# Both halves of a unit's value products behind the second pair of scores of the next unit, in the second layer of a two-layer transformer kernel

## The reference

```python
# retention layer, then latent attention + 4 experts (first layer), then:
q, k, v = (x @ Wq.T + bq, x @ Wk.T + bk, x @ Wv.T + bv)   # 16 heads of 8
scores = einsum('bhqd,bhkd->bhqk', q, k) * 8 ** -0.5       # not causal
scores[:, :, 0, -1] = scores[:, :, -1, 0] = -1e9
out = einsum('bhqk,bhkd->bhqd', softmax(scores), v)
x = layernorm(x + out @ Wo.T)
# then the ternary-weight projection and the last layernorm
```

## Time and profile before

| | us |
|---|---|
| median of 3 timed executions (lowest, highest) | 999.44 (997.81, 1001.86) |
| the profiled execution's own time | 990.96 |
| span of its trace | 989.2 |
| PE busy in it | 877.2 (89%) |
| DVE busy | 764.4 (77%) |
| ACT busy | 652.9 (66%) |
| mean granted TensorE clock, share of full | 0.971 |

### The profile page before, as it was taken

One profiled execution on the slowest core, in us unless ns is written; L12 is line 12 of the kernel. 1 busy time (PEld: TensorE's weight loads), 2 busy tenths in 40 slices (PEclk: granted clock), 3 DMA queues, 4 the chain that ended last, 5 costly groups with the idle time before them and its releaser, 6 DMA issues.

```text
span 989.2 us, 22910 instructions
## 1 busy us (share of the span) xinstructions
PE 877.2 (89%) x9098; PEld 440.9 (45%) x9098; DVE 764.4 (77%) x1156; ACT 652.9 (66%) x1285; POOL 390.4 (39%) x607
## 2 busy tenths in 40 slices
PE   8999899999778889988988779989989999999983
PEld 5777777778433343433734222336322222222232
DVE  4687676856687778879477588876889999999845
ACT  3555556566337777776456448765778878998981
POOL 3764677778443541236263112333441111111330
PEclk9999999999999999999989889999999999999996
DMA  8000000200500234012412410033106000100000
GB/s 304 1 2 1 1 2 1 76 1 2 154 21 23 79 120 117 23 57 74 135 35 94 122 31 23 10 111 96 46 29 178 21 20 21 39 2 3 5 22 22
DMA packets 49406, 52.53 MB, mean 53 GB/s; under 512 B 8874, under 2 KB 40618, under 8 KB 49140
## 3 DMA queue, kind: packets, MB, share of 16 engines
q1 hardware_dynamic: 45012, 48.12, 16.0%
q0 software_dynamic: 4288, 2.94, 1.1%
HBM read 32.37 MB, written 19.68 MB: 53 GB/s over the span
## 4 chain that ended last, share of the span: by engine, by line
PE 41%; DVE 27%; POOL 12%; issue 9%; ACT 6%; DMA 3%; SPq 2%; DVEq 0%; POOLq 0%; ACTq 0%
DVE arena L1980 19%; PE banks L1642 11%; PE banks L1607 7%; PE banks L1527 5%; ACT arena L1800 4%; POOL arena L383 2%; PE banks L1717 2%; PE banks L1725 2%; DMA arena<-arena 1%; PE banks L660 1%; POOL arena L896 1%; POOL arena L895 1%; PE banks L501 1%; PE banks L765 1%; POOL arena L386 1%
## 5 line engine op out<-in xcount | busy, mean ns | idle before, releaser
L1800 ACT ACTIVATE arena<-banks 128x512 f32<-128x512 f32 (+1 forms) x768 | 409.8, 588 | 110.4 <-PE banks L1607 79.9
L1980 DVE TENSOR_REDUCE arena<-banks 128x2 f32<-128x1024 f32 (+1 forms) x384 | 439.7, 1196 | 51.7 <-PE banks L1527 28.8
L1642 PE MATMUL banks<-arena 128*9 128x256 f32 (+1 forms) x3328 | 254.8, 382 | 5.8 <-ACT arena L1813 3.9
L1527 PE MATMUL banks<-arena 56*128 56x512 bf16 (+3 forms) x896 | 162.9, 366 | 29.4 <-DVE arena L1980 22.6
L1607 PE MATMUL banks<-arena 61*128 61x512 bf16 (+4 forms) x896 | 166.4, 371 | 23.6 <-ACT arena L1800 17.9
L1607 PEld LDWEIGHTS banks<-arena 61*128 61x128 bf16 (+1 forms) x896 | 44.2, 93 | 183.9 <-ACT arena L1800 157.2
L1383 POOL CAST arena<-arena 16x128 bf16<-16x128 f32 x32 | 8.9, 279 | 293.6 <-ACT arena L1868 289.6
L1642 PEld LDWEIGHTS banks<-arena 128*9 128x9 f32 x3328 | 51.4, 89 | 129.5 <-issue 82.9
L1527 PEld LDWEIGHTS banks<-arena 56*128 56x128 bf16 x896 | 45.0, 95 | 55.7 <-DVE arena L1980 44.7
L383 POOL TENSOR_TENSOR arena<-arena 128x8 f32<-128x8 f32 (+1 forms) x35 | 51.3, 1466 | 30.3 <-DVE arena L2144 27.9
L1393 POOL DMA_DIRECT2D arena<-arena x96 | 55.1, 577 | 10.7 <-POOL arena L1386 9.2
(11 more groups left out here) (243 smaller groups left out, 1428.6 us busy)
## 6 DMA issues: line engine op xcount, KB each, us to landing
arena<-k_products SPq DMA_DIRECT2D x32, 224.0 KB
arena<-q_products SPq DMA_DIRECT2D x64, 112.0 KB
q_products<-arena SPq DMA_DIRECT2D x16, 384.0 KB, 3.4
k_products<-arena SPq DMA_DIRECT2D x16, 384.0 KB, 3.7
arena<-e_w SPq DMA_DIRECT2D x22, 256.0 KB, 3.5
arena<-arena POOLq DMA_DIRECT2D x96, 4.0 KB, 1.8
sorted_rows<-c_pads SPq DMA_DIRECT2D x2, 709.5 KB, 8.5
arena<-sorted_rows SPq DMA_DIRECT2D x4, 258.0 KB, 3.1
```

Source lines behind the costliest of these rows:

```text
L1527: ins = nc.tensor.matmul(bank(first + par)[:, at:at + hi - lo], Qs[k_][rows, qc, y, qo:qo + P], Ks[k_][rows, y, lo:hi], start=True, stop=n ...
L1642: ins = nc.tensor.matmul(PS[h * VROWS:h * VROWS + VW, AV_BANK, o:end], V[:, b, kt, HG * g + h, :], Pr[u % PROBS][:, h, o:end], start=(kt = ...
L1800: s_.activation(Pr[s % PROBS][:, 2 * x + par, o:C], scores[:, o:C], ACT.Exp) \
L1980: v_.tensor_reduce(of[:, :, x], two_banks[:, :, 0:width], AX.X, ALU.max).then_inc(ring_dve, 1)
```

## The change

One condition in `order()` gets a case more. It says behind which of the two pairs of scores (`x`) of step `s` the half `y` of the value products of unit `s - 1` is put:

```diff
                     if 0 < s <= NU:
                         late = narrow(*us[s - 1])
-                        seq += [("V", (s - 1, y)) for y in range(2) if (0 if late else y) == x]
+                        seq += [("V", (s - 1, y)) for y in range(2) if (0 if late else y if us[s - 1][0] < BLOCKS else 1) == x]
```

## The result

The changed kernel takes 1037.5 us (median of 4 executions, 1033.2 to 1039.5), the kernel before beside it 1000.65 (997.8 to 1002.4). The ratio is 1.036, 95% interval 1.033 to 1.039: slower by about 36 us. In a second session both were faster, 1027.5 against 992.2, with a ratio of 1.034 (1.029 to 1.039). The forecast was 1032 in a range of 1019 to 1049.

A forecast was written before the change was run, and what follows sets the result against it. No single engine bounds the kernel; in the plain stage PE, VectorE and ScalarE are all nearly full. Terms 22.5 + 4 + 2 + 4 = +32.5 on the median 999.4 give 1032 us, range 1019 to 1049.

The forecast's parts named there:

- The gap of 1.14: Plain unit, first to second pair of scores: stays 1.14 us, held by the first exponential, with PE idle 0.53.
- The run of sixteen: Joined value products behind the second A pair: 1.06 us, saving 0.11 of PE time a unit.
- The plain unit: One second-layer unit without other work between: 2.67 us against 2.23, +0.44.
- The block and the plain stage: Eight units, 19.95 us before, become 22.4, +2.4; the stage from 744.9 to 930.3 has 9.3 such blocks, +22.5.
- The copy's delay: At a block's start, the first exponential waits behind the copy of the sums: 0.2 us a block, between 0.1 and 0.3.
- The last stage: From 930.3 to 961.6, 12 units without A pairs: +0.24 or +0.44 each, half and half, +4 us.
- The experts: From 656.6 to 695.8, 6 units: between +0.6 and +2.6 us, put at +2.
- The mixed stages: 586.9 to 656.6 and 695.8 to 744.9, 37 units: +1.6 if all waits vanish, +16 if none, put at +4 us.
- my own sign: Stated test for being wrong, one of three: the mixed stretches of the second layer take over 10 us more.
- The clock: Second layer: clock stays at 1.00 with PE busy 80% of a plain unit, so its term is 0.
- The rival of the swinging clock: Brief PE idle makes the clock swing to half in a quarter of 370 us: +33, 1065 us; chance 0.08.
- Absorption and gain: Two rivals: VectorE absorbs the gap, 999 us, chance 0.05; faster if the gap is below 0.70, 990 us, chance 0.04.

The follow-up runs named there:

- The short exponential: First of four exponentials in each second-layer unit cut to 256 of 512 columns: on the changed kernel 1.008, on the kernel before 0.998, both against the kernel before.
- the repeat: The changed kernel run and profiled once more with nothing altered, in a later session: 1027.5 us against 992.2, ratio 1.034 to the kernel before.
- the two kernels above with a changed first or fifth step alone: Kernel before, with both A pairs in a block's first gap: 1.002; or with half 0 ahead of the A pair in the step behind M: 0.997.

## Why the prediction was right

*The gap of 1.14.* Right: 1.13 to 1.14 in every unit of the plain stage but a block's first, which has 1.27 to 1.28; idle 0.53. It rested on reading a wait of 0.05 as a loop of 1.14 that was nearly covered. The short exponential moves the gap by as much as the instruction shrinks, and the A pairs fill it without moving it. That is shown, not only argued.

*The run of sixteen.* Right: 1.05 for 1.06, 1.53 from the second pair on. PE's busy total went down by 11 in the first profile, where I had 14; within the second layer, up to its last unit, it went down by 14.8, and outside of the layer PE was busy 3.6 more.

*The plain unit, +0.44.* Measured +0.43.

*The block and the plain stage.* I had 22.4 for a block; the repeat's trace has 22.2 to 22.3 for each of the six plain ones. The stage grew by 20.4 for 70 units, against my 22.5 for 73, which is 21.6 for 70. The copy's delay is 0.14 a block, in my 0.1 to 0.3. All waits for reductions there vanished, as worked out.

*The last stage.* +4 predicted, +3.96 measured: plain units 2.44 against 2.21, the others +0.43 to +0.44, but for one that did not grow.

*The experts.* +2 predicted, +1.3: three of the six units grew by 0.44, the other three not at all.

*The mixed stages.* +4 predicted, +6.6 measured in the repeat: this is the term that was mis-sized. I stood near the end where every wait vanishes. In the repeat the second gaps of the 39 units grew by 15.6 together and the first gaps gave back 9.0. What the first gaps last beyond 1.14 adds up to 15.1 before and to 6.2 in the repeat, so 6.2 of waiting stayed that I had let vanish. Fourteen of the units had no such wait to give (first gap 1.13 to 1.18), and they account for 5.5 of the 6.6. Others kept theirs, as this gap, which is 2.35 long before and in the repeat, and the run of sixteen came on top:

```profile
619.15 0.39 PE L1607 MATMUL banks<-arena 61*128 61x512 bf16 x2
...
621.50 0.39 PE L1607 MATMUL banks<-arena 61*128 61x512 bf16 x2 [1.74 <-ACT arena L1800]
```

By my own sign (wrong if the mixed stretches take over 10 us more) the first profile would count against me: 12.7, of which 6.1 are the pause and the units next to it. The true figure may also be a microsecond or two above 6.6. The first mixed stage took 75.87 before at a clock of 0.93; in the two kernels above with a changed first or fifth step alone it took 74.20 and 74.29 at 1.00.

*The sum.* +32.5 predicted; +32.3 in the layer in the repeat. That they meet to 0.2 is luck in part: the plain stage and the experts came out lower than I had, the mixed stages 2.6 higher. The timed difference is 35 to 37, with an interval of about 3 to 5 on either side. In the range, the lower end is worked out as 1022 and then stands as 1019; no step gives the 3 between them.

*The clock.* Full speed in the whole of the four later stages, with PE busy 160.44 of 197.72, 81%, in the plain one. The rival of the swinging clock did not happen. The Trainium skill's case of brief idle between groups ("TensorE: Matmul & The Clock Gate", "A second HAM failure mode: psum-queue depth-cycling"), in which the clock swings between its two levels, did not show here with an idle of 0.53 in every unit of 2.66. But the comparison that I rested this on was weak. It took one fall of the clock, behind a stretch with PE busy 53%. The trace of the kernel before has another, behind one with PE busy 3.33 of 3.41:

```profile
625.37:628.78 3.41, 3.33 (x39) 2.22 (x33) 2.28 (x2) 2.07 (x5) 1.05 (x4) 1.00 0.01 2
628.78:632.20 3.42, 3.42 (x25) 0.50 (x24) 3.01 (x14) 1.95 (x4) 2.06 (x4) 0.50 0.05 9
```

So the busy share alone did not tell that the clock would stay; that it stayed is shown by the runs, and why is not.

*Absorption and gain.* VectorE did not absorb the gap: it waits for the A pairs (L1527), which stand behind the gap in TensorE's list. The point from which the change would win, a gap of 0.70, was not tried; the short exponential went to 0.92 and made a unit of 2.44, in line with it.

## What to carry to other kernels

A wait of 0.05 us in a dense loop may be the visible tip of a fixed loop of more than a microsecond. Before moving work out of a gap, add up what the gap must last anyway (start to exponential, exponential, release) and compare it with what is left in it. Work moved out of a gap that another engine holds open does not shorten the gap, and its time is added elsewhere: here 0.43 a unit for a half of 0.55, since the joined run of sixteen saves 0.11. And a delay measured at one density (the copy's 0.14, with ScalarE idle 0.5 in each unit) does not hold at another, where it was 0.32.

## What the runs showed that I had not expected

The pause of 3.9 us in the first profile of the changed kernel, at 652.8, is a wait of ScalarE that the row marks as released from outside ("remote"). VectorE has such a row with 1.8 us, which ends at the same time. TensorE waited behind it, and its clock was 0.50 from 656.7 to 663.5. The pause stood in one profile of the two of that kernel. What causes it stays open.

The same kernel took 1000.65 in one session and 990.6 to 992.2 in the later ones, 0.9% apart, while its ratio to the changed one moved by 0.2%. Times across sessions are not to be compared.
